# The last batch's attention in another order on all engines: maxima of two head pairs together, scores of the last two pairs apart, odd pairs' transposes elsewhere

## The reference

```python
# layer 0
mi = einsum('bkd,od->bko', x, Wi);  mj = einsum('bkd,od->bko', x, Wj)
out = deg[None, :, None] * (mi + b) + einsum('ij,bjo->bio', a, mj)
h = layernorm(x + out)
# layer 1, 8 heads
scores = einsum('bhqd,bhkd->bhqk', q, k) * scale
scores = where(adj == 0, -inf, scores)
attn = softmax(scores)
o = einsum('bhqk,bhkd->bhqd', attn, v)
y = layernorm(h + o @ Wo.T + bo)
```

## Time and profile before

| what | value |
|---|---|
| median of 3 runs | 3103.09 us (3101.38 to 3103.33) |
| the profiled execution | 3101.49 us, its span 3099.7 us |
| TensorE busy | 3047.3 us, 98% of the span |
| VectorE, ScalarE, GpSimd busy | 66%, 54%, 37% |
| mean granted clock of TensorE | 0.993 |
| attention of batch 63 | from 3047.38 us of the span to 3086.23 us |

### The profile page before, as it was taken

The page is one execution under the profiler, slowest core; times in us unless marked ns, Lnnn a source line. Parts: engine busy times, 40 slices in busy tenths (PEclk is TensorE's granted clock), DMA queues, the critical chain, the costliest instruction groups (busy, mean ns, idle before and its releaser), DMA issues.

```text
span 3099.7 us, 59624 instructions
## 1 busy us (share of the span) xinstructions
PE 3047.3 (98%) x20480; PEld 2688.8 (87%) x20480; DVE 2035.2 (66%) x5644; ACT 1660.3 (54%) x4487; POOL 1157.2 (37%) x1097
## 2 busy tenths in 40 slices
PE   6999999999999999999999999999999999999996
PEld 5888888888888888888888888888888888888885
DVE  5666666666666666666666666666666666666665
ACT  3555555555555555555555555555555555555554
POOL 3333343333333333433333334334333333343332
PEclk8999999999999999999999999999999999999998
DMA  3101101011011011010110110110101101101000
GB/s 129 35 21 41 40 20 41 24 37 41 20 41 41 20 41 38 23 41 20 41 41 20 41 41 20 41 31 30 41 20 41 41 20 41 41 20 41 27 28 21
DMA packets 73002, 108.36 MB, mean 35 GB/s; under 512 B 3600, under 2 KB 36880, under 8 KB 72976
## 3 DMA queue, kind: packets, MB, share of 16 engines
q1 hardware_dynamic: 72976, 108.02, 10.6%
HBM read 74.46 MB, written 33.55 MB: 35 GB/s over the span
## 4 chain that ended last, share of the span: by engine, by line
PE 97%; DVE 1%; DMA 0%; ACT 0%; issue 0%; POOL 0%; SPq 0%; POOLq 0%; DVEq 0%; ACTq 0%
PE proj L339 73%; PE av L339 8%; PE attn L478 7%; PE attn L466 7%; PE proj L416 2%; DMA hb<-in_w0T 0%; DMA xb<-in_x 0%; ACT probs L612 0%; DVE h L846 0%; DVE pT_lo L793 0%; POOL xb L259 0%; DVE probs L778 0%; DVE wi_lo L898 0%; POOL var_eps_h L273 0%; DVE h L821 0%
## 5 line engine op out<-in xcount | busy, mean ns | idle before, releaser
L612 ACT ACTIVATE probs<-probs,exp_bias 128x256 f32<-128x256 f32 x1024 | 508.8, 499 | 180.3 <-DVE exp_bias L784 180.3
L281 POOL TENSOR_TENSOR oT_lo<-oT,oT_hi 128x256 fp32r<-128x256 f32 x256 | 189.3, 739 | 1040.8 <-ACT oT_hi L643 1040.8
L628 ACT CAST pT_hi<-attn 128x512 fp32r<-128x512 f32 x512 | 275.5, 591 | 457.9 <-PE av L339 253.6
L803 DVE SCALAR_TENSOR_TENSOR oT<-av,bv_cols,o_part 64x256 f32<-64x256 f32 x512 | 243.3, 475 | 379.4 <-ACT o_part L636 291.7
L248 POOL TENSOR_TENSOR probs<-probs,row_inv 128x512 f32<-128x512 f32 x256 | 263.7, 1040 | 454.1 <-DVE row_inv L789 454.1
L793 DVE TENSOR_TENSOR pT_lo<-attn,pT_hi 128x512 fp32r<-128x512 f32 x512 | 327.3, 681 | 120.5 <-ACT pT_hi L628 118.5
L636 ACT COPY o_part<-av 64x512 f32<-64x512 f32 x256 | 149.3, 583 | 479.9 <-PE av L339 478.3
L778 DVE CUSTOM_DVE_ANT_0 probs<-attn,mask_add 128x256 f32<-128x256 f32 x1024 | 372.0, 420 | 13.4 <-issue 3.3
L339 PE MATMUL proj<-mj_hi,wq_hi 128*128 128x256 f32 x1024 | 289.0, 282 | 1.5 <-DVE mj_lo L738 1.5
L339 PE MATMUL proj<-mj_hi,wq_lo 128*128 128x256 f32 x1024 | 288.9, 282 | 0.0
L339 PE MATMUL proj<-mj_lo,wq_hi 128*128 128x256 f32 x1024 | 288.7, 282 | 0.0
(11 more groups left out here) (98 smaller groups left out, 8633.0 us busy)
## 6 DMA issues: line engine op xcount, KB each, us to landing
xT_raw<-in_xT SPq DMA_DIRECT2D x64, 512.0 KB, 4.6
xb<-in_x SPq DMA_DIRECT2D x64, 512.0 KB, 5.3
out<-hb SPq DMA_DIRECT2D x64, 512.0 KB, 3.3
probs<-in_w0T SPq DMA_DIRECT2D x1, 1024.0 KB, 6.8
hb<-in_w0T SPq DMA_DIRECT2D x1, 1024.0 KB, 8.9
probs<-in_wqT SPq DMA_DIRECT2D x1, 1024.0 KB, 5.1
hb<-in_wkT SPq DMA_DIRECT2D x1, 1024.0 KB, 5.9
probs<-in_wvT SPq DMA_DIRECT2D x1, 1024.0 KB, 5.2
```

The costliest lines, as they stand in the source:

```text
L281: pool.tensor_tensor(oT_lo[:, g, :], oT[:, :], oT_hi[:, g, :].bitcast(F32), ALU.subtract).then_inc(o_split, 1)
L612: last = nc.scalar.activation(e, e, ACT.Exp, bias=exp_bias[:, g % 2, s:s + 1], scale=SCALE, accum_out=row_sum[:, g % 2, s:s + 1])
L628: nc.scalar.copy(pT_hi[:, i, :, :], attn[2 * (g % 2) + i][:, :].rearrange("p (k q) -> p k q", k=R)).then_inc(pt_hi_done, 1)
L803: last = V.scalar_tensor_tensor(out=oT[i * HALF:(i + 1) * HALF, :], in0=av[0:HALF, i * N:(i + 1) * N], scalar=bv_cols[:, 2 * g + i:2 * g + ...
```

## The change

All loops and steps but the last stay as they are. In the last step:

- VectorE takes the maxima of pairs 1 and 0 one behind the other, ahead of pair 0's inverse.
- TensorE does the second half of batch 62's output product directly behind the first, then the transposes of pairs 0 and 1, then the scores of pair 2 alone, attention 0, the scores of pair 3 alone, attention 1.
- The transposed parts of the odd pairs go to `mj_hi` and `mj_lo` instead of `pT_hi` and `pT_lo` (`pT_tail`), and the copies wait for the attention two pairs back instead of the one before.
- ScalarE, VectorE and GpSimd follow with lists of their own.

The diff, with the lists cut to a few lines:

```diff
+        pT_tail = [(pT_hi, pT_lo), tuple(t[:, :, :].rearrange("p r (a n) -> p r a n", a=2) for t in (mj_hi, mj_lo))]
...
-            def scores(b, pair, first=False):
+            def scores(b, pair, first=False, only=None):
 
                 pe.wait_ge(read["q"], 2 * b + pair + 1)
                 pe.wait_ge(read["k"], 2 * b + pair + 1)
+                pairs = (2 * pair, 2 * pair + 1) if only is None else (only,)
                 if not (first and pair == 0):
-                    pe.wait_ge(pt_read, 2 * (G * b + 2 * pair))
-                for g in (2 * pair, 2 * pair + 1):
+
+                    pe.wait_ge(pt_read, 2 * (G * b + pairs[-1] - 1))
+                for g in pairs:
...
-            def attend(b, g, first=False):
+            def attend(b, g, first=False, tail=False):
...
-                    terms = [(kt, half) for kt in range(R) for half in (pT_hi, pT_lo)]
+                    terms = [(kt, half) for kt in range(R) for half in pT_tail[g % 2 if tail else 0]]
...
                 scores(b, 0)
                 y(b - 1, 0, tail=True)
+                y(b - 1, 1, tail=True)
                 transpose_p(b, 0, 0)
                 transpose_p(b, 0, 1)
-                attend(b, 0)
                 transpose_p(b, 1, 0)
                 transpose_p(b, 1, 1)
-                y(b - 1, 1, tail=True)
-                scores(b, 1)
-                attend(b, 1)
+                scores(b, 1, only=2)
+                attend(b, 0)
+                scores(b, 1, only=3)
+                attend(b, 1, tail=True)
...
                 if i == 0 and not (first and g == 0):
-                    act.wait_ge(av_done, G * b + g)
-                nc.scalar.copy(pT_hi[:, i, :, :],
+                    act.wait_ge(av_done, G * b + g - (1 if tail else 0))
+                nc.scalar.copy(pT_tail[g % 2 if tail else 0][0][:, i, :, :],
...
                 split_o(b, 0)
+                normalise_odd(b, 2)
                 split_o(b, 1)
-                normalise_odd(b, 2)
                 normalise_odd(b, 3)
+                root("out", b - 1)
                 split_o(b, 2)
-                root("out", b - 1)
                 split_o(b, 3)
```

More of the change, by code:

```diff
@@ L622, in normalise_even, with pt_high @@
                 last.then_inc(norm_even_done, 1)
-            def pt_high(b, g, i, first=False):
+            def pt_high(b, g, i, first=False, tail=False):
                 act.wait_ge(pt_done, 2 * (G * b + g) + i + 1)
                 if i == 0 and not (first and g == 0):
-                    act.wait_ge(av_done, G * b + g)
-                nc.scalar.copy(pT_hi[:, i, :, :],
+                    act.wait_ge(av_done, G * b + g - (1 if tail else 0))
+                nc.scalar.copy(pT_tail[g % 2 if tail else 0][0][:, i, :, :],
                                attn[2 * (g % 2) + i][:, :].rearrange("p (k q) -> p k q",
@@ L708, in last_step @@
                 normalise_even(b, 1)
+                pt_high(b, 1, 0, tail=True)
+                pt_high(b, 1, 1, tail=True)
                 o_low_part(b, 0)
-                pt_high(b, 1, 0)
-                pt_high(b, 1, 1)
+                exponentials(b, 2)
                 o_high(b, 0)
-                exponentials(b, 2)
+                normalise_even(b, 2)
                 o_low_part(b, 1)
-                normalise_even(b, 2)
                 exponentials(b, 3)
+                pt_high(b, 2, 0, tail=True)
+                pt_high(b, 2, 1, tail=True)
                 o_high(b, 1)
-                pt_high(b, 2, 0)
-                pt_high(b, 2, 1)
                 normalise_even(b, 3)
                 o_low_part(b, 2)
-                pt_high(b, 3, 0)
-                pt_high(b, 3, 1)
+                pt_high(b, 3, 0, tail=True)
+                pt_high(b, 3, 1, tail=True)
                 o_high(b, 2)
@@ L789, in inverse_sums, with pt_low @@
                 V.reciprocal(row_inv[:, g % 2, :], row_sum[:, g % 2, :]).then_inc(inv_done, 1)
-            def pt_low(b, g, i):
+            def pt_low(b, g, i, tail=False):
+                high, low_ = pT_tail[g % 2 if tail else 0]
                 dve.wait_ge(pt_hi_done, 2 * (G * b + g) + i + 1)
-                V.tensor_tensor(pT_lo[:, i, :, :],
+                V.tensor_tensor(low_[:, i, :, :],
                                 attn[2 * (g % 2) + i][:, :].rearrange("p (k q) -> p k q", k=R),
-                                pT_hi[:, i, :, :].bitcast(F32), ALU.subtract).then_inc(pt_read, 1)
+                                high[:, i, :, :].bitcast(F32), ALU.subtract).then_inc(pt_read, 1)
             def o_sum(b, g, first=False):
@@ L939, in last_step @@
                 maxima(b, 0)
+                maxima(b, 1)
                 inverse_sums(b, 0)
-                maxima(b, 1)
                 y_sum(b - 1, 0, 0)
+                norm_stats("out", b - 1, 0, read["y"], hb_row[0])
                 inverse_sums(b, 1)
+                y_sum(b - 1, 1, 0)
                 pt_low(b, 0, 0)
                 pt_low(b, 0, 1)
-                norm_stats("out", b - 1, 0, read["y"], hb_row[0])
+                norm_stats("out", b - 1, 1, read["y"], hb_row[0])
+                maxima(b, 2)
+                pt_low(b, 1, 0, tail=True)
+                pt_low(b, 1, 1, tail=True)
                 o_sum(b, 0)
-                pt_low(b, 1, 0)
-                pt_low(b, 1, 1)
-                maxima(b, 2)
                 inverse_sums(b, 2)
@@ L953, in last_step @@
                 o_sum(b, 1)
+                pt_low(b, 2, 0, tail=True)
+                pt_low(b, 2, 1, tail=True)
                 inverse_sums(b, 3)
[L955 to L958, removed]
+                norm_mean("out", b - 1)
                 o_sum(b, 2)
-                norm_mean("out", b - 1)
-                pt_low(b, 3, 0)
-                pt_low(b, 3, 1)
+                pt_low(b, 3, 0, tail=True)
+                pt_low(b, 3, 1, tail=True)
                 norm_apply("out", b - 1, hb_row[0])
```

4 lines of the change are left out of this document (2 added, 2 removed).

## The result

The changed kernel takes 3095.64 us (median of 10 executions, 3093.23 to 3097.47), the kernel before 3102.39 us (median of 10, 3100.56 to 3104.72): 6.75 us less, ratio 0.9978 with a 95% interval of 0.9968 to 0.9987. The profiled execution takes 3094.08 us, its span is 3092.2 us against 3099.7. The interval is 4.0 to 9.9 us: it holds the forecast's 8.1 us, the 9.1 of rival B and the 5.1 of rival C, so the time alone can't choose among them. The traces do.

The account below looks back on a forecast made before the run. Waits along the last batch's softmax, on TensorE's chain, were taken as the bound: 6.5 + 2.65 = 9.1 us earlier, less 1.0 for the clock, is 8.1; 3103.09 - 8.1 = 3095.0 us, range 3091.5 to 3098.8.

Parts of the forecast that it names:

- rival B: Last step's first TensorE gap keeps full clock: 9.1 us gained, 3094.0; with attention 2 at full too, 10.1; chance 0.28.
- rival C: Clock returns late: attention 3 and about nine last-product matmuls at 1.2 GHz; 5.1 us gained, 3098.0; chance 0.21.
- The chain up to the scores of pair 2: Last step: earlier maxima 1 and the new TensorE order let maxima 2 start at 3061.1 instead of 3067.58, 6.5 us earlier.
- From maxima 2 to attention 2: Last step: this stretch takes 9.75 us instead of 12.4, 2.65 less, with scores 3 newly waiting for pair 1's low parts.
- 3071 to 3072 named as a sign: Last step: time at which attention 2 would start if the forecast is right, with attention 3 about 5 us later.
- The clock's term: Clock falls in the first gap, delaying exponentials 2 by 1.0 us; half clock stays at attention 2; 9.1 becomes 8.1.
- I keep 5.20: Attention 2 to attention 3 in the last step: still 5.20 us at half clock, the order being nearly the same.
- Behind attention 3 nothing moves, so the end follows it: After attention 3 in the last step: no gain or loss, so the kernel's end shifts as attention 3 does.
- D: Clock falls in the last step's first gap and never returns: 0.9 us gained, 3102.2, no change; chance 0.06.
- E: Shifted loop code adds a 0.36 us TensorE issue pause per batch, 22.7 us over 63 batches: 3117.7, slower; chance 0.03.
- the 3047 that the prediction named: End of batch 62, before the last step; an end off 3047 us was to be the sign of E.

Follow-up runs that it names:

- e3: Kernel before with the second half of the output product moved directly behind the first, TensorE's gaps filled with unread matmuls; 3098.67 us, ratio 0.9985.
- e7: Changed kernel, gaps filled, with ScalarE's copies of pair 2 ahead of exponentials 3 and GpSimd's normalisation of pair 2 ahead of pair 0's split; 3092.16 us.
- e2: Changed kernel with extra unread matmuls in TensorE's four gaps of the last step (6, 7, 12 and 7); 3092.42 us, ratio 0.9965.
- e1: Kernel before with 58 extra unread matmuls in TensorE's six gaps of the last step; 3099.04 us, ratio 0.9987.
- e6: Kernel before, gaps filled, with maxima 1 ahead of pair 0's inverse on VectorE; 3098.72 us, ratio 0.9985.
- e4: Changed kernel, gaps filled, with scores 2 and 3 again one block behind attention 0 and pair 1's low parts ahead of maxima 2; 3094.11 us.
- e5: Changed kernel, gaps filled, with the odd pairs' transposed parts back in pT_hi and pT_lo, copies waiting for the attention before; 3093.24 us, ratio 0.9968.
- e10: The kernel of e9 with extra unread matmuls also in three gaps of the first 80 us (38, 5 and 6); 3087.27 us, ratio 0.9948.
- e9: Changed kernel's last step reordered again, last output product cut by head pairs, with unread matmuls in three gaps (4, 6, 2); 3090.28 us, ratio 0.9958.

## Why the prediction was right

Forecast were 3095.0 us and 8.1 us less; measured are 3095.64 and 6.75. The chain and the clock's part in it were right up to attention 3; one term was mis-sized, the clock's return behind it, which the prediction put at nothing and which costs 1.49 us. Step by step, as distances from P (the prediction's times less 3050.36):

| step | predicted | measured |
|---|---|---|
| scores 2 | 9.5 | 9.67 |
| exponentials 2, the clock's fall included | 13.4 | 13.61 |
| attention 2 | 21.5 | 21.91 |
| attention 3 | 26.7 | 27.09 |
| first output sum of the last batch, S | 32.85 | 34.74 |

- **The chain up to the scores of pair 2.** Right. Exponentials 1 start 4.77 us behind P (3053.91 - 3049.14), predicted 4.8. The moved half of the output product cost nothing, as forecast: TensorE still waits 1.90 us for ScalarE behind it and pair 0's transposes. Done alone it gains 0.53 us (e3).
- **From maxima 2 to attention 2.** Right in its mechanism: scores 3 wait for pair 1's low parts (1.17 us, released by VectorE), and maxima 3 come right behind pair 2's inverse (3064.86), which the clock had made late, so that this wait itself cost nothing. The transposes of pair 2's second half wait 0.29 us for GpSimd (3066.98), but ScalarE's copies come only at 3069.09, so that did not count either. Exponentials 3 and the copies behind them on ScalarE then set attention 2, as e7 shows. Attention 2 is 0.4 us later than forecast, a little beyond the 3071 to 3072 named as a sign (3072.27, with the 1.22 us of the start added).
- **The clock's term.** That it falls in the first gap and takes about 1 us before exponentials 2 was right; the output copy of pair 0 at 3062.26 stands ahead of exponentials 2 at 3062.75, as put. Against e2 exponentials 2 come 13.61 - 12.54 = 1.07 us later. The prediction wrote the 0.6 us of scores 2 as half of 1.63, which would be 0.8; against e2 they took 0.4 more (1.34 us against 0.91). Half clock at attention 2 and pair 3's transposes cost 5.18 - 4.22 = 0.96, the 1.0 of the prediction. The term was mis-sized at the end. "I keep 5.20" between attentions 2 and 3 held (5.18), but "Behind attention 3 nothing moves, so the end follows it" did not: the clock came back later against attention 3 than in the kernel before, and attention 3 and the start of the last product cost 1.49 us more. This is rival C's mechanism at half of its price of 3.0: about three matmuls ran at half clock, not nine. The prediction had it as a rival with a chance of 0.21 and left it out of its sum; the gain of 6.23 us lies between the forecast's 8.1 and C's 5.1, nearer to C. By e2 the whole of the clock costs the changed kernel 3.42 us (0.96 up to attention 2, 0.96 to attention 3, 1.50 behind), and by e1 the kernel before 3.00.
- **Why the time still came out close.** From P to S the change gains 6.23 us, not 8.1; 0.4 of the missing 1.9 lie ahead of attention 3, 1.5 behind it. That the time is off by only 0.6 us is in part luck: the predicted time was counted from 3103.09, and the ten executions of before have their median at 3102.39, 0.7 lower; and the medians differ by 6.75 us, 0.5 more than the stretch from P to the end, which is within what executions differ by ahead of P.
- **Rivals.** B (first gap at full clock) fell by the slice from 3059; what it would have given e2 shows: 40.97 - 31.32 = 9.65 us from P to S, where the prediction had 10.1 for full clock in both gaps. D fell by the clock's return in 3062 and 3079. E falls too. The last step starts 1.2 us off the 3047 that the prediction named for it, but all of that is there at 90 us already: from those maxima of batch 0 to P both kernels take the same time to 0.01 us (2959.63 and 2959.64), so the loop between is not slower.

By parts, at full clock and to attention 3: maxima together 0.85 (e6), moved product 0.53 (e3), separate scores 1.59 (e4), other tiles 0.84 (e5). They add up to 3.8 of the 6.66 us between e1 and e2. For the other 2.9 there are left the orders that only work together, such as pair 1's transposes ahead of attention 0, and the lists of ScalarE and GpSimd; these were not tried alone, so that they make it up is argued, not shown, and how they share it stays open. Two of the four were measured on the kernel before and two on the changed one, so they need not add.

## What to carry to other kernels

In a last step without other work to fill the gaps, walk the chain engine by engine with each queue in mind, and price TensorE's clock in the new order down to the work behind the last gap, since a new order also moves the place at which the clock returns. Where executions spread by more than the change is worth, measure from a mark inside the program, and hold the clock with matmuls that nobody reads, cut to fit the gaps; here they paid in all three orders tried (3.00, 3.42 and 0.46 us from P to S).

## What the runs showed of the hardware

Executions of the kernel before spread over 7.5 us (3100.39 to 3107.84 in 24). In the profiles the start of the last step differs by what arises in the first 95 us, in the clock around two gaps of TensorE, of 10.08 us ahead of 38.86 and of 1.84 us ahead of 79.72 in before (PEclk 0.59 and 0.90 in the stretches shown). In e10 it is 1.00, and its five executions spread over 1.5 us where the five of e9 spread over 3.0. The same gap does not always make it fall: behind the one of 1.84 us it fell in before and in e7, and not in the changed kernel, whose gap there is as long. The Trainium skill (TensorE: Matmul & The Clock Gate, "Why this matters for your kernels") warns that the clock drops back when TensorE idles between bursts of matmuls. The runs agree that it falls in or behind such gaps, and show it for a shorter one than the page speaks of: with transposes on either side, the 1.90 us in the changed kernel's last step were enough. Filling the gaps was worth 3.00 us from P to S in the order before (e1), 3.42 in the changed one (e2), 0.46 in the new one (e9), and 3.0 us of the time at the start (e10). The extra matmuls cost nothing that shows where they ended before the wait did: in e2 TensorE still idles 0.67 and 0.47 us behind them.
